# Scaled sums of the row statistics moved off GpSimd, and the first scatters spread over four steps, in a graph-attention and mixture-of-experts kernel

## The reference

```python
# block 1: attention over a graph of 2048 nodes
xn = layernorm(x)
h = xn @ W.T + b_W
e = leaky((h @ a1)[:, None] + (h @ a2)[None, :] + b_a)      # slope 0.2
x = x + softmax(where(adj > 0, e, -9e15), axis=1) @ h
# block 2: 64 experts, the two best for each row
xf = layernorm(x)
top, idx = top_k(xf @ Wr + br, 2);  gates = softmax(top)
x = x + sum over k of gates[:, k] * (relu(xf @ W1[idx] + b1[idx]) @ W2[idx] + b2[idx])
```

## Time and profile before

| | |
|---|---|
| median of 3 runs | 277.06 us (275.08 to 278.5) |
| the profiled execution, its own time | 276.1 us |
| its span | 274.3 us |
| TensorE busy | 227.0 us (83%) |
| VectorE busy | 208.3 us (76%) |
| ScalarE busy | 180.3 us (66%) |
| GpSimd busy | 170.3 us (62%) |
| mean granted TensorE clock | 0.913 of full |

### The profile page before, as it was taken

How to read it: one execution, slowest core, us unless ns; L and a number is a source line. 1 busy time by engine, 2 the same in 40 slices (tenths; PEclk the granted TensorE clock), 3 DMA queues, 4 the chain that set the end, 5 groups by cost and what they waited for, 6 DMA issues and landing times.

```text
span 274.3 us, 6241 instructions
## 1 busy us (share of the span) xinstructions
PE 227.0 (83%) x1863; PEld 215.7 (79%) x1863; DVE 208.3 (76%) x587; ACT 180.3 (66%) x425; POOL 170.3 (62%) x212
## 2 busy tenths in 40 slices
PE   1493999999978599988775719999999999999840
PEld 1362999999978489988654609999999999999740
DVE  6899999997999739898466504889887676666455
ACT  2768889999876466867435126787877777777300
POOL 5860013562979868588887755445888888866500
PEclk9998699999997959999995557999999999999995
DMA  6999744789374870019911112232159710100067
GB/s 164 201 168 168 143 79 79 173 230 239 128 195 141 220 291 0 12 31 409 404 50 39 51 53 79 61 81 59 51 155 311 250 38 32 41 31 22 31 200 269
DMA packets 11120, 36.89 MB, mean 134 GB/s; under 512 B 2256, under 2 KB 2832, under 8 KB 10320
## 3 DMA queue, kind: packets, MB, share of 16 engines
q0 software_dynamic: 5232, 14.98, 24.4%
q1 hardware_dynamic: 5424, 21.11, 22.4%
q10 hardware_dynamic: 432, 0.40, 0.6%
HBM read 39.36 MB, written 5.51 MB: 164 GB/s over the span
## 4 chain that ended last, share of the span: by engine, by line
PE 55%; POOL 13%; DVE 12%; issue 8%; DMA 7%; ACT 3%; SPq 1%; POOLq 0%; DVEq 0%; ACTq 0%
PE bank L1148 16%; PE bank L1160 16%; PE bank L1041 11%; POOL table L431 7%; PE bank L1017 6%; DVE arena L755 3%; DMA xs<-in_x 2%; DMA arena<-result 2%; POOL rstd L414 2%; DVE arena L749 2%; PE bank L1137 2%; POOL nm L416 1%; PE bank L1060 1%; DMA rows_in<-table,arena 1%; DVE xs L825 1%
## 5 line engine op out<-in xcount | busy, mean ns | idle before, releaser
L1041 PE MATMUL bank<-arena 128*128 128x130 f32 x512 | 64.0, 283 | 0.3 <-ACT arena L578 0.2
L1041 PEld LDWEIGHTS bank<-arena 128*128 128x128 f32 x512 | 61.9, 198 | 0.8 <-issue 0.5
L1148 PE MATMUL bank<-arena 128*128 x384 | 60.5, 282 | 0.1
L1160 PE MATMUL bank<-w2s,arena 128*128 x384 | 59.0, 276 | 0.2 <-issue 0.2
L431 POOL DMA_INDIRECT table<-rows_in,pos x32 | 45.2, 1413 | 12.8 <-issue 7.8
L1148 PEld LDWEIGHTS bank<-arena 128*128 128x128 f32 x384 | 51.7, 196 | 0.5 <-issue 0.3
L1160 PEld LDWEIGHTS bank<-w2s,arena 128*128 128x128 f32 x384 | 50.9, 193 | 0.6 <-issue 0.6
L909 DVE SCALAR_TENSOR_TENSOR arena<-bank,arena 128x128 f32 x96 | 33.6, 350 | 21.8 <-PE bank L1160 19.9
L656 ACT ACTIVATE arena<-bank,arena 128x128 f32<-128x128 f32 x96 | 35.2, 367 | 18.3 <-PE bank L1148 16.9
L578 ACT ACTIVATE arena<-bank 128x512 f32<-128x512 f32 x64 | 33.9, 597 | 11.8 <-PE bank L1017 11.7
L1017 PE MATMUL bank<-ident,arena 128*128 128x128 f32 x256 | 34.3, 292 | 8.6 <-DVE arena L755 8.6
(11 more groups left out here) (195 smaller groups left out, 286.6 us busy)
## 6 DMA issues: line engine op xcount, KB each, us to landing
arena<-in_adj POOLq DMA_DIRECT2D x16, 512.0 KB, 6.4
w2s<-in_w SPq DMA_DIRECT2D x8, 768.0 KB, 4.5
arena<-in_w SPq DMA_DIRECT2D x6, 1024.0 KB, 9.7
arena<-in_w SPq DMA_DIRECT2D x4, 512.0 KB, 4.7
w2s<-in_w SPq DMA_DIRECT2D x4, 512.0 KB, 3.9
xs<-in_x SPq DMA_DIRECT2D x4, 256.0 KB, 6.2
arena<-result SPq DMA_DIRECT2D x2, 512.0 KB, 4.3
arena<-result SPq DMA_DIRECT2D x4, 256.0 KB, 5.7
```

The costliest lines, as they stand in the source:

```text
L1041: ins = pe.matmul(OB[t % 2][:, 0:D + 2], pt_r[:, t % 2, j, :], h[:, j, :], start=(j == 0), stop=(j == T - 1))
L1148: ins = pe.matmul(hp(p, b), w1u[:, p % UW, P * b:P * b + P], xT_all[:, bass.ds(column, P)], start=True, stop=True)
L1160: ins = pe.matmul(yp(p), hT[:, p % UH, b, :], w2s[:, bass.ds(u, 1), b, :].rearrange("p e d -> p (e d)"), start=(b == 0), stop=(b == HB - 1))
```

## The change

- In `rstd_of` GpSimd no longer makes the two scaled sums. VectorE makes nm2 = -total/128 right behind `residual(t)` of the last tile of each entry of `LNS` (it waits for its own sum first), and ScalarE makes ve2 right behind `deviation(t)` of that tile, as an activation with the bias `eps`, a new 128x1 tile (it waits for its own sum too). GpSimd waits for both, each at the instruction that reads it.
- The scatters of tiles 0, 1, 2, 3 stand in steps 10, 11, 12, 13; before they stood in steps 10, 10, 11, 11. Those of tiles 4 to 7 stay.

```diff
-    PLACED = [(0, 0, 10), (0, 1, 10), (0, 2, 11), (0, 3, 11), (1, 4, 14), (1, 5, 15), (1, 6, 15), (1, 7, 15)]
+    PLACED = [(0, 0, 10), (0, 1, 11), (0, 2, 12), (0, 3, 13), (1, 4, 14), (1, 5, 15), (1, 6, 15), (1, 7, 15)]
...
+        eps = sb("eps", [P, 1])
...
+        s_neg = sem("s_neg")
...
+            pool.memset(eps[:, :], EPS)
...
             def rstd_of(i):
                 t0, t1 = LNS[i]
-                pool.wait_ge(s_spread, t1)
-                pool.tensor_scalar(nm2[:, t0:t1], total[:, t0:t1], -1.0 / D, None, ALU.mult)
-                pool.tensor_scalar(ve2[:, t0:t1], spread[:, t0:t1], 1.0 / D ** 3, EPS, ALU.mult, ALU.add).then_inc(s_ve2, 1)
                 pool.wait_ge(s_ve2, i + 1)
                 pool.tensor_tensor(rstd2[:, t0:t1], ve2[:, t0:t1], expo[:, t0:t1], ALU.pow).then_inc(s_rstd2, 1)
                 pool.wait_ge(s_rstd2, i + 1)
+                pool.wait_ge(s_neg, i + 1)
                 pool.tensor_tensor(nm2[:, t0:t1], nm2[:, t0:t1], rstd2[:, t0:t1], ALU.mult).then_inc(s_nm2, 1)
...
                 act.activation(off[:, :], xs[:, t, :], ACT.Square, bias=total[:, t:t + 1], scale=-float(D),
                                accum_out=spread[:, t:t + 1]).then_inc(s_spread, 1)
+                for t0, t1 in LNS:
+                    if t == t1 - 1:
+                        act.wait_ge(s_spread, t + 1)
+                        act.activation(ve2[:, t0:t1], spread[:, t0:t1], ACT.Identity, bias=eps[:, 0:1], scale=1.0 / D ** 3).then_inc(s_ve2, 1)
...
                 dve.scalar_tensor_tensor(xs[:, t, :], OB[t % 2][:, 0:D], rinv[:, t:t + 1], xs[:, t, :],
                                          ALU.mult, ALU.add, accum_out=total[:, t:t + 1]).then_inc(s_x1, 1)
+                for t0, t1 in LNS:
+                    if t == t1 - 1:
+                        dve.wait_ge(s_x1, t + 1)
+                        dve.tensor_scalar(nm2[:, t0:t1], total[:, t0:t1], -1.0 / D, None, ALU.mult).then_inc(s_neg, 1)
```

## The result

The changed kernel takes 267.49 us (median of 4, 266.82 to 267.81), the kernel before in the same session 276.07 us (274.4 to 278.5). The ratio is 0.972, with a 95% interval of 0.966 to 0.978: faster by 2.8%. The ratio is of fast runs alone, those within 1.5% of the quickest of their kernel, and leaves out the 278.5 us of before. The forecast was 2.4% (270.3 against 277.06). The profiled execution is 9.28 us shorter than that of before (266.82 against 276.1), its span 9.2 us; the forecast was 6.8 us, with 8.2 in the better case. The runs also scatter less: 1 us where the kernel before has 4.

A forecast was written before the change was run, and what follows sets the result against it. Bound: the path rstd_of(3) to top2(1), and GpSimd's queue from tile 4 on. leaky(15)'s scatter ends 5.4 us earlier and the work behind is 1.4 us shorter: 6.8 us, so 270.3 us median; range 267.9 to 273.9.

The forecast's parts named there:

- the better case: rstd_of(5) gets through before scores(15), so norm(10) doesn't wait: gain 8.2 us, 268.9 us; counted into the forecast's 0.62.
- Part 1: Tile 1's scatters leave step 10: rstd_of(3) ends earlier, the stall before route_a(1) goes; gain 5.6 us at pos(1).
- Part 2: Nine sums on VectorE at 0.2 us each, partly hidden in idle time; net gain at leaky(15) 5.4 us.
- Part 3: Nine sums as activations on ScalarE, 0.32 us each with the gap; up to step 9 evac(6), route_a(0) 0.1 to 0.3 us later.
- Part 4: Three shorter rstd_of calls on GpSimd after leaky(15): 1.76 us less, minus a 0.35 us wait for ScalarE, net 1.4 us.
- Part 5: Scatters moved to steps 12 and 13: tile 3 fits before tile 4, through near 106.9, using up 3.38 us of idle time.
- rival 1: rstd_of(5) beats scores(15): leaky(15)'s 1.02 us and some 0.4 of queue go; 8.2 us, 268.9; within the forecast's 0.62.
- Rival 2: Held GpSimd calls give back gain at tile 4, 271.4 us; if VectorE also waits for moved scatters, 273.9; chance 0.21.

The follow-up runs named there:

- e10: Kernel before plus one VectorE instruction behind the residual of tile 11, a scaled copy of row sums into an unread tile; ratio 0.997.
- e1: Kernel before with only the scatters moved (tiles 0 to 3 in steps 10 to 13), scaled sums left on GpSimd; 272.62 us, ratio 0.991.
- e2: Changed kernel with the scatters back in the old order (steps 10, 10, 11, 11), so only the sums moved; 268.41 us, ratio 0.975.
- e12: Changed kernel with the old scatter order and both scaled sums on ScalarE, none on VectorE; 269.64 us, ratio 0.980.
- e4: Changed kernel with the sums off GpSimd only for tiles 0 to 11; 270.08 us, ratio 0.982.
- e6: Changed kernel with the scatters of tiles 1, 2, 3 in steps 12, 13, 13; 271.68 us, ratio 0.988.
- e8: Kernel before plus nine VectorE instructions behind residuals, scaled copies of row sums into an unread tile, nothing taken from GpSimd; ratio 1.002.

## Why the prediction was right, and where it was not

- **The bound** was read rightly: both places named, the path to `top2(1)` and GpSimd's queue from tile 4 on, are where the time went, 6.99 us and 2.65 us.
- **Part 1.** `top2(1)` was forecast at 95.4 and came at 95.34, with the clock at 1.00; pos(1) near 106.4, and it came at 105.96; `norm(6)` "near 90.5", and it started at 90.34. Counted from the first residual, which came 0.37 us later than before, these are 0.4 to 0.8 us early. The 5.6 us at pos(1) took the slow clock, and the 0.97 us behind it, as consequences of the stall; e10 shows that the same stall can come without them, so 2.4 of the 5.6 us belong to the execution that was profiled. That they came true together is in part luck. The cause, too, was too narrow. The order of tile 1's scatters is enough to remove the stall (e1), and so is the removal of two small instructions (1.02 us of 3.95 left in e2, 1.78 in e12, where VectorE has no added instruction). I had credited those with 0.59 us at `rstd_of(3)`. What was missing is that each of them is one more instruction that a pass can hold for 2 us, and that a later end of one decides over the next.
- **Part 2.** 0.2 us for each instruction on VectorE: from the start of `scores(10)` to that of `scores(11)` it took 5.79 us where it took 5.55, so 0.24. Those of the first three odd tiles hid in the 1.29 us before `top2(0)`, of which 0.45 were left. Right.
- **Part 3.** 0.30 us, forecast 0.32. Right.
- **Part 4.** The three shorter calls are worth 1.65 us in B by e4; the forecast was 1.4, with a wait of 0.35 that was 0.43. Right. B shrank by a further microsecond (2.65 in all), since one scatter fewer was left after `leaky(15)`.
- **Part 5.** Tile 3 was through at 106.93 and tile 4's first scatter started at 107.23, as worked out (106.9, before 107.5). Right, and narrow: e6 shows 4 us on the other side.
- **The term that was mis-sized** is the 1.02 us of `leaky(15)`, which the sum left in and rival 1 took out. It went, and with it a whole scatter of 1.27 us from the queue behind, where rival 1 had 0.4 (8.2 in all, 9.2 measured). The step that failed is the judgement that this branch "hangs on tenths" and is therefore the less likely one. It does hang on tenths, and the changed kernel and the ones with short calls everywhere are on the good side, by 1.1 us here (the last call starts at 112.67, `scores(15)` at 113.75) and by 0.13 us with both sums on ScalarE. The bad side is worth 3.76 us, not the 1.02 of before.
- **Rival 2's half about the port** (VectorE waiting 0.9 us for each scatter) did not come about: line 760 has a mean of 2352 ns against 2348. The scatter that began at 92.25, 0.12 us ahead of `leaky(11)`, took 0.96 us, and the pass beside it 2.34.

## What to carry to other kernels

Where long passes of another engine can hold an engine's instructions, the cost of one is not its duration but its duration plus the chance of being held by the other engine's next pass; four small instructions of 0.2 to 0.7 us in a row lasted 7.7 us in e8. Count separate instructions, and move or merge them first, before you reorder big ones. When you cost a move, lay the new queue along the other engine's passes and note each place where a start is within a few tenths of a pass's start: there the estimate has two values, and the edit may buy or lose a whole pass. A shorter hold alone buys nothing if the next instruction is caught in its place.

## What the runs showed of the hardware

- A scatter that starts just after a VectorE pass with two SBUF inputs can still get through. In the changed kernel the one at 80.97 began 0.05 us after `leaky(9)` (80.92) and took 0.98 us, while the pass took 2.38 us in place of 2.35; one at 86.59 beside a pass of 86.50 took 1.05 us, and the pass 2.41. The Trainium skill (SBUF — State Buffer, Who interferes with whom) has the loser block fully until the winner's instruction ends. The traces agree for starts 0.13 us or more into a pass: in all fourteen profiles, each scatter that began so in a pass of the attention loop up to `leaky(15)` ended 0.8 to 1.0 us behind it; for these two it shows no full block on either side, only 0.03 to 0.06 us. In the other direction it doesn't agree: `leaky(11)` took 2.34 us beside a scatter that had begun first.
- The edge is not sharp. Of 16 scatters that began 0.01 to 0.09 us into a pass, 15 got through, and the one in e12, 0.09 us behind `leaky(11)`, was held for the whole pass:

```profile
92.05 2.35 DVE L761 SCALAR_TENSOR_TENSOR arena<-arena,tneg 128x2048 f32<-128x2048 f32 x1
```
```profile
92.14 3.18 POOL L432 DMA_INDIRECT table<-rows_in,pos  x1 [0.17 <-issue]
```

- After TensorE's gap of 2.2 to 2.4 us before `turn(9)`, the 16 transposes take 3.2 to 3.6 us in nine of the fourteen profiles (3.52 in the changed kernel's) and 1.97 us in the other five, the granted clock between 81 and 87.5 us being 0.74 and 1.00, as these rows of the changed kernel and of the one with both sums on ScalarE show:

```profile
81.00:87.50 6.50, 4.15 (x23) 4.15 (x24) 6.46 (x9) 4.49 (x9) 5.60 (x5) 0.74 0.75 152
```
```profile
81.00:87.50 6.50, 4.42 (x40) 4.42 (x41) 6.46 (x8) 5.82 (x12) 6.12 (x5) 1.00 0.59 171
```

The same instructions with the same idle time before them meet either of the two levels, 1.2 or 2.4 GHz. The transposes alone make up to 1.5 us of A between kernels (84.57 and 83.74 are with the fast one, 85.79 and 86.01 with the slow one), and so the A of single profiles doesn't settle differences of a microsecond. The clock behind the stall of 3.38 us differs in the same way: 0.62 in the profile of before, 1.00 in e10's. What decides it wasn't tried.
